# Routed experts of an audio tower: the expert's weights as stationary operand, fetched for each tile of tokens into a ring of three

## The reference

```python
scores = jnp.einsum('bnc,ce->bne', x, gate_w) + gate_b
p_experts = jax.nn.softmax(scores - gate_center, axis=-1)
expert = jnp.argmax(p_experts, axis=-1).reshape(-1)
xt = x.reshape(-1, c)                                   # c = 192
h = jax.nn.gelu(jnp.einsum('tc,ech->eth', xt, w1) + b1[:, None, :], approximate=False)   # 768 hidden
out_all = jnp.einsum('eth,ehc->etc', h, w2) + b2[:, None, :]
out = jnp.take_along_axis(out_all, expert[None, :, None], axis=0)[0]
```

## Time and profile before

| | |
|---|---|
| median of three runs | 2660.51 us (2659.21 to 2662.45) |
| the profiled execution | 2663.34 us, of which the span is 2661.5 us |
| PE busy over the span | 2278.3 us (86%) |
| DVE, ACT, POOL busy | 1424.6, 1120.0, 868.1 us |
| granted TensorE clock, mean | 0.926 of full speed |
| DMA over the span | 104.89 MB, 39 GB/s in the mean |

### The profile page before, as it was taken

How to read it: one execution, slowest core, us unless ns; L and a number is a source line. 1 busy time by engine, 2 the same in 40 slices (tenths; PEclk the granted TensorE clock), 3 DMA queues, 4 the chain that set the end, 5 groups by cost and what they waited for, 6 DMA issues and landing times. The chain is left out here.

```text
span 2661.5 us, 47737 instructions
## 1 busy us (share of the span) xinstructions
PE 2278.3 (86%) x16381; PEld 2047.0 (77%) x16381; DVE 1424.6 (54%) x3624; ACT 1120.0 (42%) x2142; POOL 868.1 (33%) x758
## 2 busy tenths in 40 slices
PE   0999999999999999999976644796997888868878
PEld 0899999999999999999965334585554656657878
DVE  6565656565666666666645882233674555531112
ACT  0556565656565656566542001111433454422210
POOL 3455554545454545455522223201220000000000
PEclk9999999999999999999987765898998999869989
DMA  1000000000000000000000013100000110027766
GB/s 53 5 3 4 3 3 3 3 4 3 4 3 4 3 4 3 4 3 4 3 2 1 0 63 98 57 19 24 17 14 5 43 47 35 35 96 251 252 194 209
DMA packets 66016, 104.89 MB, mean 39 GB/s; under 512 B 9589, under 2 KB 52255, under 8 KB 64861
## 3 DMA queue, kind: packets, MB, share of 16 engines
q1 hardware_dynamic: 51102, 80.77, 9.4%
q10 hardware_dynamic: 9280, 14.00, 1.6%
q0 software_dynamic: 5568, 9.27, 1.2%
HBM read 75.44 MB, written 28.49 MB: 39 GB/s over the span
## 5 line engine op out<-in xcount | busy, mean ns | idle before, releaser
L255 PE MATMUL bank<-t_wt,t_l 128*128 128x128 f32 x8508 | 1043.0, 276 | 4.1 <-ACT t_l L330 2.9
L255 PEld LDWEIGHTS bank<-t_wt,t_l 128*128 128x128 f32 x8508 | 1012.4, 193 | 18.1 <-ACT t_l L330 3.9
L426 POOL TENSOR_TENSOR t_rstd<-t_var,t_minus_half 128x4 f32<-128x4 f32 (+1 forms) x379 | 366.6, 967 | 626.5 <-DVE t_var L355 626.5
L363 DVE TENSOR_TENSOR t_yn<-bank,t_rstd 128x512 f32<-128x512 f32 (+1 forms) x379 | 249.1, 657 | 344.6 <-POOL t_rstd L426 325.9
L312 ACT ACTIVATE t_sq<-bank 128x512 f32<-128x512 f32 (+1 forms) x379 | 215.9, 570 | 480.1 <-PE bank L255 477.8
L432 POOL TENSOR_TENSOR t_zrstd<-t_zvar,t_minus_half 128x8 f32<-128x8 f32 x196 | 320.8, 1638 | 43.1 <-DVE t_zvar L390 43.1
L343 ACT ACTIVATE t_l<-bank,t_cols 128x512 f32<-128x512 f32 x384 | 292.7, 778 | 47.6 <-PE bank L302 41.9
L352 DVE TENSOR_REDUCE t_ss<-t_sq 128x4 f32<-128x512 f32 (+1 forms) x379 | 244.3, 645 | 111.5 <-ACT t_sq L312 111.4
L330 ACT ACTIVATE t_l<-bank,t_cols 128x512 f32<-128x512 f32 (+2 forms) x381 | 285.1, 748 | 10.7 <-PE bank L264 5.9
L264 PE MATMUL bank<-t_ident,t_yn 128*128 128x128 f32 x1426 | 219.4, 274 | 11.5 <-DVE t_yn L363 10.3
L264 PEld LDWEIGHTS bank<-t_ident,t_yn 128*128 128x128 f32 x1426 | 173.5, 141 | 25.3 <-DVE t_yn L363 11.3
(11 more groups left out here) (316 smaller groups left out, 3474.5 us busy)
## 6 DMA issues: line engine op xcount, KB each, us to landing
t_w<-in_w SPq DMA_DIRECT2D x64, 480.0 KB
ect<-t_ECT SPq DMA_DIRECT2D x16, 750.0 KB, 3.2
t_ectb<-ect ACTq DMA_DIRECT2D x5, 1500.0 KB, 7.8
t_w1x<-in_w1x SPq DMA_DIRECT2D x64, 97.5 KB
ys<-t_ye SPq DMA_DIRECT2D x64, 96.0 KB
t_yb<-ys ACTq DMA_DIRECT2D x8, 768.0 KB, 10.8
t_ectb<-ect POOLq DMA_DIRECT2D x12, 375.0 KB, 6.2
t_xs<-in_x SPq DMA_DIRECT2D x50, 82.5 KB, 1.8
```

What stands on the lines that cost most here:

```text
L255: mm = pe.matmul(psY[bank][:, t * C:(t + 1) * C], src[:, at:at + P], T["wt"][:, 3 * (layer - 1) + k, :], start=(k == 0), stop=(k == 2))
L363: dve.tensor_tensor(T["yn"][:, par, 0:n * C].rearrange("p (t c) -> p t c", c=C), psY[bank][:, 0:n * C].rearrange("p (t c) -> p t c", c=C), ...
L426: pool.tensor_tensor(T["rstd"][:, par, 0:n], T["var"][:, par, 0:n], T["minus_half"][:, 0:n], ALU.pow)\
```

## The change

The hidden activations are produced already transposed, and the weights no longer live in SBUF.

- `w1a`, `w1b` and `w2` shrink from four experts to a ring of FFN_RING = 3 slots. For each tile SP reads the tile's expert into a register and issues three transfers (393 KB, 197 KB and 590 KB, 1.18 MB in all) into slot i % 3. From the fourth tile on it first waits for `routed_out` of tile i - 3. The stores stand between the loads in SP's order.
- In up, the weights are the stationary operand and the tile moves: twelve products of 128 columns in place of four of 384. The result has the hidden features on partitions.
- The first bias is then one value for each partition. It is loaded once as `b1T`, by a transfer whose source has a stride and whose runs are of one element (3072 of them), and ACT adds it: six activations of 128 columns for a tile in place of two of 384.
- turn_hidden and copy_hidden are gone; the banks freed give the transposed rows (`pX`) and the output (`pO`) two banks each. PE's order is up(i), turn_rows(i+1), down(i-1).
- In `gate`, the loads of the weights are gone and that of `b1T` is added.

```diff
@@ gate, sync
-            for name in ("w1a", "w2", "upper", "steps"):
+            for name in ("upper", "steps"):
                 sp.dma_start(T[name][:], io[name]).then_inc(S["weights_loaded"], 16)
-            sp.dma_start(T["w1b"][HIGH, :], io["w1b"][0:D2, :]).then_inc(S["weights_loaded"], 16)
+            src = bass.AP(io["w1b"].tensor, D2 * N_EXPERT * HID, [[1, P], [P, N_EXPERT * HC], [1, 1]])
+            sp.dma_start(T["b1T"][:, :].rearrange("p (n o) -> p n o", o=1), src, allow_slow_non_contiguous=True)\
+                .then_inc(S["weights_loaded"], 16)
...
@@ routed_ffn, sync
+            def load_weights(i):
+                slot = i % FFN_RING
+                if i >= FFN_RING:
+                    sp.wait_ge(S["routed_out"], i - FFN_RING + 1)
+                e = sp.value_load(T["expert"][0:1, i:i + 1], min_val=0, max_val=N_EXPERT - 1)
+                hidden = bass.ds(e * HID, HID)
+                done = S[f"ffn_loaded{slot}"]
+                sp.dma_start(w1a[:, slot, :], io["w1a"][:, hidden]).then_inc(done, 16)
+                sp.dma_start(w1b[HIGH, slot, :], io["w1b"][0:D2, hidden]).then_inc(done, 16)
+                sp.dma_start(w2[:, slot, :], io["w2"][:, bass.ds(e * (HC * D), HC * D)]).then_inc(done, 16)
...
+            for i in range(FFN_RING):
+                load_weights(i)
             sp.wait_ge(S["scattered"], 16 * TILES)
             for n in range(len(LOADS)):
                 s = slice(starts[n], starts[n + 1])
                 sp.dma_start(r[:, s, :], rows[:, s, :]).then_inc(S[f"routed_loaded{n}"], 16)
...
+            for i in range(FFN_RING, ROUTED):
+                load_weights(i)
+                if i - FFN_RING + 1 in starts:
+                    store(starts.index(i - FFN_RING + 1) - 1)
+            store(len(LOADS) - 1)
@@ routed_ffn, tensor
             def up(i):
-                expert[i] = pe.value_load(T["expert"][0:1, i:i + 1], min_val=0, max_val=N_EXPERT - 1)
+                slot = i % FFN_RING
+                pe.wait_ge(S[f"ffn_loaded{slot}"], 16 * PARTS_W * (i // FFN_RING + 1))
                 pe.wait_ge(S["rows_copied"], i + 1)
...
-                    pe.matmul(o, eA[:, i % 2, :], T["w1a"][:, w], start=True, stop=False)
-                    pe.matmul(o, eB[:, i % 2, :], T["w1b"][:, w], start=False, stop=True).then_inc(S["hidden_done"], 1)
...
+                        pe.matmul(o, w1a[:, slot, w], eA[:, i % 2, :], start=True, stop=False)
+                        mm = pe.matmul(o, w1b[:, slot, w], eB[:, i % 2, :], start=False, stop=True)
...
             turn_rows(0)
-            for i in range(ROUTED + 2):
+            for i in range(ROUTED + 1):
                 if i < ROUTED:
                     up(i)
-                if 1 <= i <= ROUTED:
-                    turn_hidden(i - 1)
                 if i + 1 < ROUTED:
                     turn_rows(i + 1)
-                if i >= 2:
-                    down(i - 2)
+                if i >= 1:
+                    down(i - 1)
@@ routed_ffn, scalar
-                    act.activation(G[:, i % 2, n * HALF_H:(n + 1) * HALF_H], pH[i % 2][n][:, 0:HALF_H], ACT.Gelu)\
-                        .then_inc(S["hidden"], 1)
+                    for c in range(HC // 2):
+                        at = n * (HC // 2) + c
+                        ins = act.activation(G[:, i % 2, at * P:(at + 1) * P], pH[i % 2][n][:, c * P:(c + 1) * P], ACT.Gelu,
+                                             bias=T["b1T"][:, bass.ds(e * HC + at, 1)])
+                    ins.then_inc(S["hidden"], 1)
```

More of the change, by code:

```diff
@@ L1164 @@
 LOADS = [3, 6, 6, 6, 6]
+FFN_RING = 3
 def routed_ffn(nc, T, S, io):
     ps = T["ps"]
[L1170 to L1171 removed]
+    pH, pX, pO = (ps[0:2], ps[2:4]), (ps[4], ps[5]), (ps[6], ps[7])
+    r, eA, eB, G = T["routed"], T["eA"], T["eB"], T["G"]
+    w1a, w1b, w2, b2 = T["w1a"], T["w1b"], T["w2"], T["b2"]
     HALF_H = HID // 2
+    PARTS_W = 3
     starts = [sum(LOADS[:n]) for n in range(len(LOADS) + 1)]
@@ L1178, in _, with store @@
         def _(sp):
+            def load_weights(i):
[8 more added lines that the diff above has]
+                sp.dma_start(w2[:, slot, :], io["w2"][:, bass.ds(e * (HC * D), HC * D)]).then_inc(done, 16)
+            def store(n):
+                s = slice(starts[n], starts[n + 1])
+                sp.wait_ge(S["routed_done"], starts[n + 1])
+                sp.dma_start(outs[:, s, :], r[:, s, :]).then_inc(S["routed_stored"], 16)
+            for i in range(FFN_RING):
+                load_weights(i)
             sp.wait_ge(S["scattered"], 16 * TILES)
@@ L1238, in down @@
+                    mm.then_inc(S["hidden_done"], 1)
+            def down(i):
+                e = pe.value_load(T["expert"][0:1, i:i + 1], min_val=0, max_val=N_EXPERT - 1)
+                pe.wait_ge(S["hidden"], 2 * (i + 1))
+                if i >= 2:
+                    pe.wait_ge(S["routed_done"], i - 1)
+                o = pO[i % 2][:, 0:D]
                 for c in range(HC):
-                    pe.matmul(pO[:, 0:D], GT[:, i % 2, c * P:(c + 1) * P],
-                              T["w2"][:, bass.ds(expert[i] * (HC * D) + c * D, D)], start=(c == 0), stop=False)
@@ L1241, in down @@
-                pe.matmul(pO[:, 0:D], T["one"][:, :], T["b2"][:, bass.ds(expert[i] * D, D)], start=False, stop=True)\
+                    pe.matmul(o, G[:, i % 2, c * P:(c + 1) * P], w2[:, i % FFN_RING, c * D:(c + 1) * D],
+                              start=(c == 0), stop=False)
+                pe.matmul(o, T["one"][:, :], b2[:, bass.ds(e * D, D)], start=False, stop=True)\
                     .then_inc(S["routed_out"], 1)
             turn_rows(0)
-            for i in range(ROUTED + 2):
+            for i in range(ROUTED + 1):
@@ L1269, in copy_rows @@
                     dve.wait_ge(S["hidden_done"], 2 * (i - 1))
[L1270 to L1277, removed]
-                    dve.tensor_copy(GT[:, i % 2, n * HALF_H:(n + 1) * HALF_H], pGT[n][:, 0:HALF_H])\
-                        .then_inc(S["hidden_copied"], 1)
+                dve.tensor_copy(eA[:, i % 2, :], pX[i % 2][:, 0:P])
+                dve.tensor_copy(eB[D2:P, i % 2, :], pX[i % 2][D2:P, P:2 * P]).then_inc(S["rows_copied"], 1)
             def copy_out(i):
                 dve.wait_ge(S["routed_out"], i + 1)
-                dve.tensor_copy(r[:, i, :], pO[:, 0:D]).then_inc(S["routed_done"], 1)
+                dve.tensor_copy(r[:, i, :], pO[i % 2][:, 0:D]).then_inc(S["routed_done"], 1)
             phi_link = Link(dve, S["phi_link"])
@@ L2021, in program @@
         late_names += ("zero_ready cleared one_ready ffn_var ffn_root scattered ranks_ready expert_ready rows_ready "
-                       "routed_done routed_stored rows_copied rows_turned hidden hidden_done hidden_copied "
-                       "hidden_turned routed_out mix_ahead0 mix_ahead1 mix_ahead2 gathered0 gathered1 gathered2 gathered3 gathered4 gathered5 gathered6 gathered7 routed_loaded0 "
+                       "routed_done routed_stored rows_copied rows_turned hidden hidden_done ffn_loaded0 ffn_loaded1 ffn_loaded2 "
+                       "routed_out mix_ahead0 mix_ahead1 mix_ahead2 gathered0 gathered1 gathered2 gathered3 gathered4 gathered5 gathered6 gathered7 routed_loaded0 "
                        "routed_loaded1 routed_loaded2 routed_loaded3 routed_loaded4").split()
```

56 lines of the change are left out of this document (19 added, 37 removed).

## The result

The kernel with the change takes 2680.84 us (median of six runs, 2676.42 to 2693.56) against 2659.0 us (six runs, 2657.0 to 2662.45) for the kernel before: a ratio of 1.0091, with a 95% interval of 1.0074 to 1.0107. It is slower by 0.9%, where the sum of the forecast, 8.2 us less, had made it 0.3% faster, and it lies outside the range of 2643 to 2667 us. The profiled execution took 2681.36 us, its span 2679.6.

The account below looks back on a forecast made before the run. PE was taken to bound the routed stage. A stage gain of 9.2 us less 1 us for stores gave -8.2 us: 2652.3 us against the median of 2660.5 (2655.1 for a profiled execution), range 2643 to 2667.

Parts of the forecast that it names:

- C: PE's work for one routed tile (up, row transposes, down): 2.68 + 0.22 + 2.28 = 5.18 us.
- E(i+2) = E(i) + L + C: Routed stage, E(i) being the end of down(i): every second tile waits 0.7 us, a pair costs 11.04 us.
- L: Time from the end of down to the next usable weights: 5.86 us, from 5.2 to 6.7.
- that case: Rival, routed stage: loads all hidden, no waits, if L is 5.18 us or less; -17.4 us, 2643.1; chance 0.12.
- that rival: Load of `b1T` delays `gate`, deciding from 35 us; at 0.25 us a run +13 us, 2665; chance 0.06.
- D: From SP's first issue to landing of a tile's 1.18 MB: 5.1 us, ends 4.55 and 5.6.
- 1180/335 = 3.5 us for the flow: Part of D beyond the fixed 1.55 us: 1.18 MB moving at the full-flow rate of 335 GB/s.
- a rival with 0.20: Slow load: load slower than the tile at up of every second tile; at 250 GB/s +6.2 us, 2666.7; chance 0.20.
- the stores, 1 us in all: Stores behind loads in SP's order, sharing the engines: 1 us in all, ends 0 and 6.3 us.
- the clock, treated as a rival beside the others: Half clock after each PE gap in the routed stage: 1.6 us a pair, 19 us, 2671; chance 0.07.
- A gap of 0.7 keeps the clock: PE's waits of 0.7 us at every second routed tile leave the clock at 1.00, costing nothing more.
- The read on SP: SP's read of the expert and address arithmetic, behind its wait: 0.4 us, from 0.3 to 0.7.

Follow-up runs that it names:

- the ring of four: Changed kernel with FFN_RING = 4 in place of 3, nothing else but one more semaphore; 2640.45 us against 2657.51 for the kernel before, ratio 0.9939.
- the runs above: Changed kernel with weights as contiguous blocks in DRAM: 1.0110 to the kernel before; the same with w1a and w2 packed into one transfer: 2676.94 us, 1.0060.
- the run with the read ahead: Changed kernel with SP reading the tile's expert before its wait for routed_out, real routing kept; 2671.73 us, ratio 1.0049 to the kernel before.

## Why the prediction was wrong

**Right.** PE's part: C is 5.17 us, forecast 5.18, so the transposes' 0.65 us a tile did go. The rule E(i+2) = E(i) + L + C, the alternation of a free and a waiting round, and the place of the wait, at up for the DMA of `w2`. That ACT, the scatter beside the first three loads, and the drain are no cost: E(1) is 1697.6 for 1696.7 (0.9 of it from before `gate`), and the ring of four, in which nothing waits, ends the stage 15.4 us earlier, forecast 17.4 for that case. The bias transfer: SP issues the next DMA 2.2 us behind it (1586.82 and 1588.99 us), it is held at `phA` for 5.08 us where the earlier trace rows had 15.06, the scatter starts on time, and that rival is refuted. The Trainium skill (DMA: Bandwidth & Descriptors, Rules for kernel authors) says that a strided last dimension lowers to one descriptor for each element; the trace agrees, as the DMA view and the stretch between 1587.8 and 1590.3 us of the kernel after show for the 3072 elements:

```profile
DMA packets 3201, 0.05 MB, mean 20 GB/s; under 512 B 3187, under 2 KB 3200, under 8 KB 3201
1587.80:1590.30 2.50, 0.00 (x0) 0.00 (x0) 2.43 (x16) 0.00 (x0) 2.50 (x7) 0.50 0.75 20
```

They took 2.5 us, not the 11 that the forecast took for them, and delayed nobody here.

**Wrong: the flow in D, the term that carries most.** The first waiting round has L = 7.42 us for the forecast's 5.86, and over 12 pairs that is 18.7 of the 34.4 us by which the stage missed (E(25) - E(1) of 166.9 for 132.5). Of the 1.56, D is 1.31 (6.41 for 5.1); 0.13 is the issue after E (0.89 for 0.16 + 0.20 + 0.4), and 0.11 the slower first product behind a wait, which had been left out. In D the fixed part of 1.55 us was right, as 1.61 us are without bytes. The failed step is 1180/335 = 3.5 us for the flow: it took 4.80 us, 246 GB/s in the mean. The 335 came from a single microsecond, and only the 590 KB of `w2` flowed so, at 333 in the difference between two runs; those of `w1a` and `w1b` had 210. The row of 252 GB/s over 40 us of the soft experts, under the same kind of load, was at hand, was used only for a rival with 0.20, and gave D = 6.3, L = 7.06: nearly what came, and with the right step. The Trainium skill's formula (same page, Anatomy of one DMA, fitted on another issue path) would make D 4.7 us, an estimate of 2.0 fixed and 2.7 of flow; the trace disagrees by 1.7, with 1.6 and 4.8. Why the first half of the load flows so slowly stays open: it is not the strided source and not the spread of the issues, by the runs above, and `w1b` was not tried by itself.

**Wrong: the stores, 1 us in all.** They cost 6.3 us of waits between two executions. That this is just the upper end that stood in the text is luck, as that end was a sum of transfer times. The argument was that a store is issued after the three issues of a load, and that the next load comes later. But a store issued 0.49 us after `w2` shares the flow with it, and `w2` lands later for it, as the D of 7.2 to 7.9 against 6.3 shows.

**Wrong: the clock, treated as a rival beside the others.** "A gap of 0.7 keeps the clock" is true, and so was each row about it. But the clock hangs on L: the same missing microsecond that makes the wait longer brings it to a length behind which the clock fell in part of the cases, and so does a store. In the kernel after, no wait up to 1.70 us cost the clock, of the nine from 1.93 to 3.39 us six did, at 1.4 to 1.6 us each and once 3.0; in the run with the read ahead one of 1.82 did and one of 2.88 did not, so no one length divides them. Together 10.5 us. So three cases that the text priced one by one, each as if it excluded the others, came at the same time: 12 x 1.56 = 18.7, another 5.4 of waits beyond the first pair's L (with the stores, above), and 10.5 of clock, less 0.2 as C was 0.01 shorter, sum to the 34.4 us. The range should have held at least the slow load with the stores at their upper end and the clock gone, and its 2667 did not: 2666.7 with 5.3 more for the stores is 2672.0, and the clock comes on top. Even the forecast's own rival of the clock, 2671, lay outside it.

The Trainium skill (TensorE: Matmul & The Clock Gate, HAM oscillation) describes a kernel in which the wait for each next slice of an operand lets the clock fall, so that each slice starts at half speed. The trace agrees for a part of the waits only: a clock of 0.50 stands behind the one of 2.74 us, but after 1.98 and 2.83 us PE ran on at the full clock.

**The read on SP** was forecast at 0.4 us, from 0.3 to 0.7, and took 0.86 in all: 0.69 between the wait and the first issue and 0.16 in D. "It is wrong if SP's read takes over 0.7 us" was the right thing to look for; in L it is the smallest of the errors, as the 0.36 us assumed around it were 0.20, and the cheapest to mend.

## What to carry to other kernels

Count a ring's slots by the time between the release of a slot and its next use, not by their number: with PE's order up(i), down(i-1), three slots left one tile of 5.17 us to a load of 7.4 us, and a fourth turned an end of the stage 26.1 us later than before into one 15.4 us earlier. Take the rate of such a load from the mean over a whole stretch of the same kind of load, not from its best microsecond. And remember that where the ring leaves no slack, whatever stands between the wait and the issue on the loading queue, here a register read and its arithmetic of 0.69 us, lengthens the wait, and so does a store issued between loads. And where TensorE's waits are as long as those behind which the traces show 1.2 GHz (here some of those from 1.8 us up), price the clock together with the wait, not as an alternative: a few tenths off the wait can then bring more than themselves, here 16.5 us in the stage between two profiled executions for 6.3 us of waits.

## What the runs showed that had not been expected

- Moving SP's read of a register value ahead of its wait took 0.55 us off each load and 15.3 us off the rounds from E(1) to E(25) (151.6 where they were 166.9: E(1) = 1698.20 and E(25) = 1849.8), since it also spared most of the half clock. By the ratios, the whole time fell by 11 us.
- Four products of no use in each gap, 31 us of PE in all, made the stage 8 us shorter.
- A load of 1.18 MB had its DMA engines busy for 1.07 and 0.85 of two neighbouring microseconds while they moved 186 and 214 GB/s, after 372 GB/s at 0.95. Over 120 us of the ring of four it was 235 GB/s at 0.84.
